# Layer 0 of two images run inside the scan stage of the two images before them, in pieces per scan step

## What is computed

```
dt = softplus(dt_raw + bias)          # dt_raw, B and C are products of x with weights
h[n] = exp(dt * A[n]) * h[n] + (dt * x) * B[n]
y = sum over n of h[n] * C[n]
```

## Time and profile before

| | |
|---|---|
| median of 3 runs | 23642.33 us (23635.3 to 23661.84) |
| profiled execution: its own time | 23647.01 us |
| profiled execution: span, mean granted PE clock | 23645.2 us, 0.738 |
| busy: PE, DVE, ACT, POOL | 18035.3, 19747.9, 9462.4, 16017.7 us |
| DMA | 2571.14 MB, mean 109 GB/s |

### The profile page before, as it was taken

One profiled execution on the slowest core, in us unless ns is written; L12 is line 12 of the kernel. 1 busy time (PEld: TensorE's weight loads), 2 busy tenths in 40 slices (PEclk: granted clock), 3 DMA queues, 4 the chain that ended last, 5 costly groups with the idle time before them and its releaser, 6 DMA issues. The chain is left out here.

```text
span 23645.2 us, 289556 instructions
## 1 busy us (share of the span) xinstructions
PE 18035.3 (76%) x82840; PEld 6320.8 (27%) x82840; DVE 19747.9 (84%) x21684; ACT 9462.4 (40%) x14504; POOL 16017.7 (68%) x8708
## 2 busy tenths in 40 slices
PE   8999999997888677777777777777777777777711
PEld 5555565552222111111111111111111111111111
DVE  4555545446666899999999999999999999999977
ACT  3333333334444344444444444444444444444400
POOL 0000000004444899999999999999999999999956
PEclk9999999998888666666666666666666666666655
DMA  0000000004554656556655655655665565565588
GB/s 17 15 14 14 14 15 14 14 14 173 183 186 174 134 122 127 125 121 127 127 122 125 127 123 123 126 126 121 126 127 122 124 127 124 121 128 125 110 202 191
DMA packets 977931, 2571.14 MB, mean 109 GB/s; under 512 B 65622, under 2 KB 324056, under 8 KB 955296
## 3 DMA queue, kind: packets, MB, share of 16 engines
q1 hardware_dynamic: 976800, 2559.04, 47.2%
HBM read 1974.33 MB, written 584.45 MB: 108 GB/s over the span
## 5 line engine op out<-in xcount | busy, mean ns | idle before, releaser
L1107 POOL TENSOR_TENSOR c_pr<-c_hs,c_c_u 128x784 f32<-128x784 f32 x6144 | 11218.2, 1848 | 760.6 <-DVE c_hs L1071 760.6
L1014 ACT ACTIVATE c_psum<-c_dt_u,c_a_neg 128x784 f32<-128x784 f32 x6144 | 5642.0, 918 | 8506.9 <-DVE c_hs L1071 8462.4
L960 PE MATMUL c_psum<-c_pr,c_red 128*64 128x392 f32 x24576 | 8085.5, 779 | 0.9 <-POOL c_pr L1107 0.9
L1071 DVE TENSOR_TENSOR_SCAN c_hs<-c_psum,c_carry,c_dbx 128x784 f32<-128x784 f32 x3456 | 6273.1, 1846 | 0.0
L951 PE MATMUL c_psum<-c_br_u,c_sel 48*128 48x512 bf16 (+1 forms) x9216 | 3373.8, 461 | 3703.3 <-DVE c_dbx L1051 3626.2
L1051 DVE TENSOR_TENSOR c_dbx<-c_u_u,c_psum 128x784 f32<-128x784 f32 x4608 | 4391.4, 953 | 51.6 <-PE c_psum L951 51.6
L177 POOL TENSOR_TENSOR a_xpb<-a_x_sb,a_pb_sb 98x768 f32<-98x768 f32 x128 | 231.1, 1806 | 5070.5 <-DVE a_x L262 5057.0
L960 PEld LDWEIGHTS c_psum<-c_pr,c_red 128*64 128x64 f32 x24576 | 1924.0, 192 | 3748.4 <-issue 2031.7
L1096 POOL TENSOR_TENSOR c_dbp<-c_u_u,c_bp_u 128x784 f32<-128x784 f32 x1536 | 2849.7, 1855 | 39.8 <-DMA c_c_u<-scr_bc 39.8
L951 PEld LDWEIGHTS c_psum<-c_br_u,c_sel 48*128 48x128 bf16 x9216 | 565.3, 103 | 8504.1 <-DVE c_dbx L1051 8009.1
L1071 DVE TENSOR_TENSOR_SCAN c_hs<-c_psum,c_carry,c_dbp 128x784 f32<-128x784 f32 x1152 | 2133.5, 1852 | 0.0
(11 more groups left out here) (105 smaller groups left out, 17490.3 us busy)
## 6 DMA issues: line engine op xcount, KB each, us to landing
c_c_u<-scr_bc SPq DMA_DIRECT2D x512, 1568.0 KB, 26.6
c_dt_u<-scr_dt SPq DMA_DIRECT2D x512, 588.0 KB, 7.3
c_u_u<-scr_u SPq DMA_DIRECT2D x512, 588.0 KB, 10.8
c_bp_u<-scr_bc SPq DMA_DIRECT2D x512, 392.0 KB, 20.2
scr_dt<-p_dt_o SPq DMA_DIRECT2D x128, 1176.0 KB, 4.5
scr_u<-p_u_o SPq DMA_DIRECT2D x128, 1176.0 KB, 5.6
scr_y<-c_y_sb SPq DMA_DIRECT2D x512, 294.0 KB, 14.4
d_yin<-scr_y SPq DMA_DIRECT2D x64, 2352.0 KB, 25.9
```

Source lines behind the costliest of these rows:

```text
L960: mm = pe.matmul(Y(3 * w + q)[64 * h:64 * h + 64, :], red[:], pr[:, s % RP, HT * h:HT * h + HT], start=(p == 0), stop=(p == NPR - 1))
L1014: nc.scalar.activation(dA(s), dt_u[:, d, s // NPR, :], ACT.Exp, scale=a_neg[:, k, s:s + 1]).then_inc(exp_done, 1)
L1071: nc.vector.tensor_tensor_scan(hs[:, s % RH, way], dA(s)[:, way], data, init, ALU.mult, ALU.add).then_inc(scan_done, 1)
L1107: nc.gpsimd.tensor_tensor(pr[:, s % RP, :], hs[:, s % RH, :], c_u[:, d, s % NPR, :], ALU.mult).then_inc(prod_done, 1)
```

## The change

Images are taken in groups of GROUP = 2. The program is now: layer 0 of images 0 and 1; then for each group prep, followed by the scan. For all groups but the last the scan is the new `build_merged`, which also runs layer 0 of the next group; the last group has `build_scan`. `build_output` comes once at the end. That makes 8 prep stages, 7 merged, one scan. Semaphores are made once (`signals`) and shared by the repeated stages, so waits count on with `ROUND` or with absolute image numbers.

In `build_merged` a chunk has CT = 448 positions (7 per image and order, so WI = 28 items and 672 steps per image); every PSUM operand is one bank: four slots for the B product, of which those of POOL_STEPS hold the decay instead, one bank for Y, three (A, B, G) for layer 0. `times_b` multiplies in place in PSUM; the decay of a DVE step lies in SBUF (`da_t`, ring of 5). POOL_PAIRS are (1, 4, 7). Layer 0 is cut into pieces: at global step 84·j + k each engine does piece k of unit j, and for k below 17 also piece k + 84 of unit j−1. The copies of v (L242) and of the transposed probabilities (L254, L255) move from DVE to ACT, in 12 instructions per unit; the softmax does one instruction for all windows of the unit where it did four; the GELUs come in two groups of three, each with its own table loads.

In both scans y is folded: the forward and the backward direction of an order visit the same chunk at different times, the first visit keeps its sum in `y_sb` (which has a place per chunk), the second starts its accumulation with a matmul of an identity (`same`) by `y_sb`, and only the second is stored. `ysc` is half as large; the output stage loads half as much y, and one POOL addition with a strided operand replaces one on POOL and two on DVE (L1206, L1228, L1232).

In `build_prep` on POOL two `hold`s become plain waits, and the wait for `bc_done` moves in front of two others.

```diff
+        def opens(w):
+
+            return w % (2 * NCHK) < NCHK
...
             def store(b, w, v):
                 o, cc, d = unit_of(w)
+                if opens(w):
+                    return
                 hold(sp, y_evac, 3 * v + 3, fence)
                 for h in range(2):
                     t0 = CT * cc + HT * h
-                    sp.dma_start(yrow[bass.ds(2 * b + o, 1), d, :, t0:t0 + HT].rearrange("u (q p) t -> p (u q) t", p=64),
-                                 y_sb[64 * h:64 * h + 64, d]).then_inc(y_out[d], 16)
+                    sp.dma_start(yrow[bass.ds(2 * (b + base) + o, 1), :, t0:t0 + HT].rearrange("u (q p) t -> p (u q) t", p=64),
+                                 y_sb[64 * h:64 * h + 64, cc]).then_inc(y_out[cc], 16)
 
...
                 if p == 0:
                     after(pe, y_evac, 3 * v + q - 1)
+                    if not opens(w):
+                        pe.matmul(Y(3 * w + q), same[:], y_sb[:, unit_of(w)[1], q, :], start=True, stop=False)
                 pe.wait_ge(prod_done, STEPS * v + s + 1)
                 for h in range(2):
                     mm = pe.matmul(Y(3 * w + q)[64 * h:64 * h + 64, :], red[:], pr[:, s % RP, HT * h:HT * h + HT],
-                                   start=(p == 0), stop=(p == NPR - 1))
...
+def build_merged(nc, tag, made, l0_io, scan_io, xn, dts, us, bcs, bps, ysc, base, n_img):
...
+    CT, HT, NCHK = 448, 224, 7
+    POOL_PAIRS = (1, 4, 7)
+    DVE_PAIRS = tuple(p for p in range(NPR) if p not in POOL_PAIRS)
+    WI = 4 * NCHK
+    STEPS = 3 * NPR
+    MULS = 3 * len(DVE_PAIRS)
+    GPS = 3 * len(POOL_PAIRS)
+    RH, RP, RD, RG, RS = 6, 6, 5, 3, 4
+    LEAD, AHEAD, LAG = 3, 2, 4
+    N_IN = 16 * 9
+    PERIOD = WI * STEPS // UW
+    END = 101
+    N0 = UW * n_img
+    ROUND = base // n_img + 1
+    END_IMG = base + n_img
...
+        slot = lambda s: ps[:, s % RS, 0:CT]
+        Y = ps[:, 4, 0:HT]
+        A, B, G = 5, 6, 7
...
+        def decay(w, s):
+
+            if s in POOL_STEPS:
+                return slot(s)
+            return da_t[:, (MULS * w + DVE_STEPS.index(s)) % RD, :]
...
+        def layer0(piece, b, w, s, first):
+
+            j, k = divmod(STEPS * w + s, PERIOD)
+            if k + PERIOD < END and not (first and j == 0):
+                piece(UW * b + j - 1, k + PERIOD)
+            piece(UW * b + j, k)
+
+        def drain(piece):
+
+            for k in range(PERIOD, END):
+                piece(UW * END_IMG - 1, k)
...
+            def piece(u, k):
+                if k == 30:
+                    hold(sp, xh_done, 2 * u + 1, fence)
+                    hold(sp, xpb_done, u + 1, fence)
+                    if not (isinstance(u, int) and u == UW * END_IMG - 1):
+                        load_x(u + 1)
+                elif k == END - 1:
+                    hold(sp, x1_done, 2 * u + 2, fence)
+                    dst = xn[:, :, bass.ds((u + N0) * UT + SHIFT * IMG, UT)].rearrange("a p t -> p a t")
+                    sp.dma_start(dst, x1T[:]).then_inc(x1_out, 16)
...
+            def spread(b, w, s):
+
+                if s in POOL_STEPS:
+                    return
+                d = w % 2
+                if s == 0:
+                    pe.wait_ge(u_in[d], in_of(b, w))
+                after(pe, scan_done, STEPS * (WI * b + w) + s - RS + 1)
+                pe.matmul(slot(s), sel[:, s % NPR, :], br_u[:, d, :], start=True, stop=True).then_inc(b_full, 1)
+
+            def reduce(b, w, s):
+                v, p, q = WI * b + w, s % NPR, s // NPR
+                if p == 0:
+                    after(pe, y_evac, 3 * v + q)
+                    if not opens(w):
+                        pe.matmul(Y, same[:], y_sb[:, unit_of(w)[1], q, :], start=True, stop=False)
+                pe.wait_ge(prod_done, STEPS * v + s + 1)
+                for h in range(2):
+                    mm = pe.matmul(Y[64 * h:64 * h + 64, :], red[:], pr[:, s % RP, HT * h:HT * h + HT],
+                                   start=(p == 0 and opens(w)), stop=(p == NPR - 1))
+                mm.then_inc(red_done, 1)
...
+            def mlp_in(u, m):
+                bank = (G, A, B)[m % 3]
+                for a in range(2):
+                    mm = pe.matmul(ps[:, bank, 0:UT], w1_sb[:, a, 128 * m:128 * m + 128], h2T[:, a, :],
+                                   start=(a == 0), stop=(a == 1))
+                mm.then_inc(h_full, 1)
...
+                elif k in (78, 79, 80):
+                    pe.wait_ge(af_done, 4 * u + 4)
+                    mlp_in(u, k - 78)
+                elif k in (84, 85, 86):
+                    pe.wait_ge(gelu_done, MC * u + k - 83)
+                    mlp_in(u, k - 81)
+                elif k in (90, 91, 92):
+                    pe.wait_ge(gelu_done, MC * u + MC)
+                    mlp_out(u, 0, k - 90)
+                elif k in (95, 96, 97):
+                    pe.wait_ge(x1_done, 2 * u + 1)
+                    mlp_out(u, 1, k - 95)
...
+            def body(b, first, last):
+                for w in range(WI):
+                    for s in range(STEPS):
+                        if not (last and w == WI - 1 and s + LEAD >= STEPS):
+                            spread(*step(b, w, s + LEAD))
+                        if s >= LAG:
...
+            def evacuate(b, w, q):
+                v = WI * b + w
+                o, cc, d = unit_of(w)
+                act.wait_ge(red_done, STEPS * v + NPR * q + NPR)
+                if q == 0 and opens(w):
+                    after(act, y_out[cc], 32 * (2 * b + o))
+                nc.scalar.activation(y_sb[:, cc, q, :], Y, ACT.Copy).then_inc(y_evac, 1)
...
+                if s in POOL_STEPS:
+                    after(act, scan_done, n - RS + 1)
+                else:
+                    i = DVE_STEPS.index(s)
+                    back = DVE_STEPS[i - RD] if i >= RD else DVE_STEPS[i - RD] - STEPS
+                    after(act, scan_done, STEPS * v + back + 1)
...
+            def gelus(u, i):
+                for m in range(3 * i, 3 * i + 3):
+                    act.wait_ge(h_full, MC * u + m + 1)
+                    nc.scalar.activation(g_sb[:, m, :], ps[:, (G, A, B)[m % 3], 0:UT], ACT.Gelu,
+                                         bias=b1_sb[:, m:m + 1]).then_inc(gelu_done, 1)
+                nc.scalar.preload_act_table_set(LN_EXP)
...
+                elif k == 82:
+                    after(act, m2_full, 2 * u)
+                    gelus(u, 0)
+                elif k == 88:
+                    gelus(u, 1)
+                elif k == 94:
+                    after(act, x1_out, 16 * u)
+                    result(u, 0)
+                elif k == 99:
+                    result(u, 1)
...
+            def times_b(b, w, s):
+
+                if s in POOL_STEPS:
+                    return
+                d, v, i = w % 2, WI * b + w, DVE_STEPS.index(s)
+                dve.wait_ge(b_full, MULS * v + i + 1)
+                if s == 0:
+                    dve.wait_ge(u_in[d], in_of(b, w))
+                nc.vector.tensor_tensor(slot(s), slot(s), u_u[:, d, s // NPR, :], ALU.mult).then_inc(mul_done, 1)
...
+                dve.wait_ge(exp_done, n + 1)
+                if s in POOL_STEPS:
+                    i = POOL_STEPS.index(s)
+                    dve.wait_ge(bp_done, GPS * v + i + 1)
+                    data = dbp[:, (GPS * w + i) % RG, way]
+                else:
+                    i = DVE_STEPS.index(s)
+                    dve.wait_ge(mul_done, MULS * v + i + 1)
+                    data = slot(s)[:, way]
+                after(dve, prod_done, n - RH + 1)
+                if s % 3 == 0:
+                    after(dve, carry_done, NPR * v + s // 3 - 1)
+                init = 0.0 if w % (2 * NCHK) < 2 else carry[:, d, s:s + 1]
+                nc.vector.tensor_tensor_scan(hs[:, s % RH, way], decay(w, s)[:, way], data, init,
+                                             ALU.mult, ALU.add).then_inc(scan_done, 1)
...
+            def unit_norm(src, t0):
+                for t in (t0, t0 + 1):
+                    ins = nc.vector.tensor_scalar(xhat[:, t, :], src[:, t, :], mv[:, t, 0:1], rstd[:, t:t + 1],
+                                                  ALU.subtract, ALU.mult)
+                return ins
...
+                    dve.wait_ge(rs_done, 2 * u + 1)
+                    after(dve, tr_done, 2 * u)
+                    unit_norm(x_sb, 0)
+                elif k == 7:
+                    unit_norm(x_sb, 2).then_inc(xh_done, 1)
...
+                    dve.wait_ge(rec_done, u + 1)
+                    nc.vector.tensor_tensor(prob[:], prob[:], rs[:].unsqueeze(3).to_broadcast([128, 3, UW, WT]),
+                                            ALU.mult).then_inc(prob_done, 1)
...
+            def body(b, first, last):
+                for w in range(WI):
+                    for s in range(STEPS):
+                        scan(b, w, s)
+                        if not (last and w == WI - 1 and s + AHEAD >= STEPS):
+                            times_b(*step(b, w, s + AHEAD))
```

(34 more changed lines are left out.)

623 lines of the change are left out of this document (562 added, 61 removed).

## The result

| | before | after |
|---|---|---|
| median | 23646.44 us (4 runs) | 24091.58 us (4 runs, 24013.54 to 24149.94) |
| ratio | | 1.0188, 95% interval 1.0166 to 1.021 |
| profiled span, granted clock | 23645.2 us, 0.738 | 24137.2 us, 0.696 |

A forecast was written before the change was run, and what follows sets the result against it. DVE and POOL, equally full, were to bound the merged stage: 1.53 + 0.085 + 0.065 = 1.68 us per step, 9408 steps, 15805 us. With 6576 for everything else that made 22380 us, range 21100 to 24000.

The forecast's parts named there:

- Layer 0 in front, prep, last scan, output: Stages outside the merged ones: 715 us for two images' layer 0, 320 per prep, 1881 and 920.
- Entry and exit of a merged stage: Time of each merged stage besides its steps: 72 us, times 7 = 504 us.
- DVE and POOL per step: Merged step: each engine has 1.53 us of work, both equally full; with mutual waiting DVE has 1.615.
- Mutual waiting, 0.085: Merged step: DVE's xhat and division wait with POOL, 7 us per unit, 0.085 us per step on DVE.
- ACT and the gelu blocks: Merged stage: ACT 1.03 us per step, hidden on average; each 4.3 us GELU block just covered by decays leading 4.8.
- rival 3: More stalls: gelu blocks outlast the decays and clusters cost twice, step 1.76 us, kernel 23130; chance 0.15.
- Queues and DMAs: Merged stage: loads, stores and SP's holds cost nothing; 3.9 MB per work item in 40 us.
- 5.5 us per unit, 0.065 per step (bounds 0 and 0.2): Merged step: DVE stalls from low-clock PE clusters, four or five per unit at 1 to 2 us, and from ACT.
- Its clusters: 18 layer-0 PE pieces (mlp_in, mlp_out, qk, values) in 28 steps, from k = 78 to the next unit's 22.
- the mean of 0.65 would give 1.04/0.65 = 1.60, just beside DVE: Merged step: PE needs 1.04 us at 2.4 GHz, 2.05 at 1.2; at the earlier scan's mean clock, 1.60.
- Rival 1: PE at 1.2 GHz sets the pace, from mean clock 0.57 down; at 0.55 kernel 24360 us; chance 0.16.
- break-even of 1.814 a step: Merged step time in us from which the change loses: (23642 − 6576)/9408.

The follow-up runs named there:

- e2: Changed kernel with layer 0 of all images in its own stage in front, so no layer-0 pieces in the merged stages: 25167.02 us.
- e4: Changed kernel with GELU replaced by the identity and the table loads left out in the merged stages: 24230.71 us.
- e8: Changed kernel with the MLP's weights and activations in bf16 in the merged stages (lower precision): 22730.4 us.
- e3: Changed kernel with 12 of the 24 MLP matmuls per unit left out in the merged stages: 23397.67 us.
- e7: Changed kernel with two idle matmuls on zeros added before each spread in the merged stages: 23180.84 us.
- e5: Changed kernel with layer-0 matmuls of q, k, v, projection, MLP and residual cut to 16 columns in the merged stages: 23690.39 us.
- e10: e8 with two idle matmuls on zeros before each spread: 22367.13 us, ratio 0.9456.
- e14: e10 with q, k, v and projection in bf16 as well (lower precision): 22078.69 us, ratio 0.9333.
- e6: Changed kernel with DVE's layer-0 instructions in the merged stages cut to 16 columns (softmax: one window of 24): 23753.36 us.
- e12: e2 with two idle matmuls on zeros before each spread: 25185.26 us.
- e9: Edits of e5 and e7 together, against the changed kernel: 22843.37 us, ratio 0.9646, clock 0.784.

## Why the prediction was wrong

- **Layer 0 in front, prep, last scan, output: right** within 1% (714, 318, 1880, 916 us against 715, 320, 1881, 920). Entry and exit of a merged stage took 61 us, not 72, which is 77 us of the kernel.
- **DVE and POOL per step: right.** POOL's product 1.13 us against 1.10, its sum 1.535 against 1.57; DVE 1.567 against 1.615. A POOL-bound step without pieces takes 1.504 (e2).
- **Mutual waiting, 0.085: mechanism right, size half.** 4 us per unit instead of 7.
- **ACT and the gelu blocks: harmless.** Without table loads nothing is gained (e4); rival 3 named the wrong engine first.
- **Queues and DMAs: nothing,** as priced. In the window of 1500 to 2500 us no wait of DVE or POOL for a load is among the large ones.
- **The step that failed: "5.5 us per unit, 0.065 per step (bounds 0 and 0.2)" for PE's stalls.** It measured 24 us, 0.28, above the upper bound. Three things were wrong in it. Its clusters were the 18 pieces of MLP, q, k and v; 14.2 us stand behind those, but 9.6 stand behind transposes, attention and projection, which the prediction had in its mean load and gave no stall. It counted four or five stalls of 1 to 2 us a unit from the low level, part of them hidden behind other waits, where the low level is there 65% of the time. And the sum judged PE by a mean clock: "the mean of 0.65 would give 1.04/0.65 = 1.60, just beside DVE".

The mean hides what happens. The clock isn't 0.68 at any moment; it is 0.50 for some 55 us and 1.00 for some 40. At 0.50 a step of PE is 2.05 us by the prediction's own sum, far above DVE's 1.615, and in a spell of 55 us, some 27 steps, a spread that leads by three steps is soon late. An estimate in this spirit: take the slower engine at each level, 2.05 and 1.615, and add the rates. With the window's 0.68 (64% low) that is 0.64/2.05 + 0.36/1.615 = 0.535 steps per us, 1.87 us a step, where 1.877 was measured; with the 0.65 that the prediction had from the earlier trace rows it gives 1.90, 24450 us. For e8 (12 × (2.98 − 0.86) = 25 us per unit less at the low level, so 1.75 for 2.05) it gives 1.70 (measured 1.73), for e3 (18 less: 1.84, at a clock of 0.66) 1.76 (1.80), for e7 (1.25 matmuls of 0.37 a step more, 2.52, but low only 20% of the time) 1.74 (1.78).

**That the totals fit is in part luck.** Each level can be counted by itself, by the starts of the recurrences. Over the seven stages of the changed kernel a step takes 1.98 us in the low spells and 1.72 in the high ones, not 2.05 and 1.615; the two errors cancel. In e3 it is 1.89 and 1.63, in e8 1.84 and 1.55. In e7 it is 1.84 and 1.76, where the estimate had 2.52 and 1.615: its low spells last only 10 us in the median, and most of its waits for spreads, 12.8 of 16.5 us per unit, stand at the full clock. So the estimate is fair where spells are long and wrong in its terms where they are short. It isn't a clean test either, since low and high spells lie at different steps of the period and so carry different pieces.

- **Rival 1, "PE at 1.2 GHz sets the pace", is nearest to what happened,** though not at its own point: it was to decide from a mean clock of 0.57 down, and the kernel lost at 0.68, because that point too was worked out from the mean. What was held against it, that a full PE runs at 0.97 in layer 0 and so "saturation should lift it", is false here: PE was full for 40 us at 0.50. A quarter of the waits, 5.9 of 23.9 us per unit, stand at the full clock and are not rival 1 but the lumps of the load themselves.
- The break-even of 1.814 a step was right: e5, at 1.82 by the same count (72 us off each stage), came out at 23690, about the time of before.

**Shown:** that PE being late costs the time (e3, e8, e10, e14 against e4, e6); that the granted clock is part of the cause (e7 faster with more work, e12 unmoved, e5 losing its saving; three quarters of the waits stand at 1.2 GHz). **Open:** what makes the clock fall and return; how much a steady full clock alone would give; e9's 0.78; why one idle matmul loses. Spreading the pieces of the MLP and the attention over more steps, and a longer lead for spreads, weren't tried.
